# Two-layer cross attention in float32 on one core: a weight split one iteration later, the mask flag read at the end of TensorE's first iteration, and the order of the first and last iterations laid out anew

## The reference

```
# layer 0, 32 x (128 channels, 512 positions)
x_q = w_qk y;  x_k = w_qk x;  x_v = w_v x + b_v
attention = softmax(x_q^T x_k);  attention /= 1e-07 + column sums
x = x + relu(w_t (x - x_v attention) + b_t)
# layer 1, 32 x (128 rows, 512), 8 kv heads, 4 groups, head size 16
q = x Wq + bq;  k = ctx Wk + bk;  v = ctx Wv + bv
scores = q k^T / 4 + mask;  out = softmax(scores) v
x = layernorm(out Wo + bo + x) * gamma + beta
```

## Time and profile before

| | us |
|---|---|
| median of 3 runs | 802.6 |
| the three runs | 800.09, 802.60, 805.04 |
| profiled execution | 796.82 |
| its span, first to last instruction | 795.0 |
| busy: PE, DVE, POOL, ACT | 738.7, 598.1, 574.8, 479.4 |

### The profile page before, as it was taken

The page is one execution under the profiler, slowest core; times in us unless marked ns, Lnnn a source line. Parts: engine busy times, 40 slices in busy tenths (PEclk is TensorE's granted clock), DMA queues, the critical chain, the costliest instruction groups (busy, mean ns, idle before and its releaser), DMA issues.

```text
span 795.0 us, 17333 instructions
## 1 busy us (share of the span) xinstructions
PE 738.7 (93%) x5015; PEld 605.0 (76%) x5015; DVE 598.1 (75%) x1016; ACT 479.4 (60%) x1067; POOL 574.8 (72%) x770
## 2 busy tenths in 40 slices
PE   6778999999999999999999999999999999998762
PEld 5766786878878788878878788887878887886521
DVE  5676795868789596877969686878969687786742
ACT  5744747567574847657493856757484765746250
POOL 4946478686887968686896868688796868657154
PEclk9989999999999999999999999999999999999786
DMA  6524161433526152342515144342615234242510
GB/s 235 173 68 110 61 156 41 131 101 100 135 76 169 45 139 85 119 109 91 156 63 152 66 123 105 102 133 79 168 47 139 82 119 109 90 107 74 123 66 27
DMA packets 55755, 84.86 MB, mean 107 GB/s; under 512 B 9520, under 2 KB 29616, under 8 KB 55600
## 3 DMA queue, kind: packets, MB, share of 16 engines
q1 hardware_dynamic: 55008, 84.25, 36.7%
q10 hardware_dynamic: 720, 0.27, 0.2%
HBM read 24.72 MB, written 8.39 MB: 42 GB/s over the span
## 4 chain that ended last, share of the span: by engine, by line
PE 81%; DMA 7%; DVE 3%; issue 3%; POOL 3%; ACT 1%; SPq 1%; POOLq 0%; DVEq 0%; ACTq 0%
PE banks L784 8%; PE banks L875 8%; PE banks L888 6%; DMA qstack<-mrep 5%; PE banks L822 4%; PE banks L900 4%; PE banks L846 4%; PE banks L823 4%; PE banks L824 4%; PE banks L902 4%; PE banks L901 4%; PE banks L769 4%; PE banks L771 4%; PE banks L770 4%; PE banks L757 3%; PE banks L758 3%
## 5 line engine op out<-in xcount | busy, mean ns | idle before, releaser
L1526 DVE TENSOR_REDUCE maxima<-banks 128x4 f32<-128x512 f32 x256 | 160.0, 683 | 9.7 <-PE banks L846 7.7
L1183 ACT ACTIVATE prob<-banks 128x512 f32<-128x512 f32 x256 | 134.9, 608 | 40.6 <-PE banks L875 39.5
L1551 DVE RECIPROCAL dens<-dens 128x512 f32<-128x512 f32 x32 | 107.1, 3348 | 60.0 <-DMA dens<-sides 60.0
L549 POOL TENSOR_TENSOR ta<-ta,cb_s 128x516 f32<-128x516 f32 x64 | 76.5, 1197 | 100.0 <-ACT ta L1125 100.0
L784 PE MATMUL banks<-ta,att 128*128 128x130 f32 x1024 | 122.0, 278 | 3.1 <-POOL ta L556 3.1
L784 PEld LDWEIGHTS banks<-ta,att 128*128 128x128 f32 x1024 | 119.6, 193 | 5.2 <-POOL ta L556 3.3
L1117 ACT ACTIVATE att<-banks,negmax 128x512 f32<-128x512 f32 x128 | 88.7, 715 | 20.7 <-DVE negmax L1476 20.4
L1476 DVE TENSOR_REDUCE negmax<-banks 128x1 f32<-128x512 f32 x128 | 85.7, 687 | 12.4 <-PE banks L771 12.3
L875 PE MATMUL banks<-qstack,kstack 128*128 128x512 f32 x256 | 80.9, 421 | 11.7 <-DMA qstack<-mrep 11.2
L1168 ACT ACTIVATE qh<-banks,bq_s 128x256 fp32r<-128x256 f32 x64 | 30.7, 480 | 99.0 <-PE banks L824 99.0
L822 PE MATMUL banks<-x2h,wq_h 128*128 128x256 f32 x256 | 73.9, 289 | 0.7 <-POOL x2l L616 0.7
(11 more groups left out here) (145 smaller groups left out, 1972.6 us busy)
## 6 DMA issues: line engine op xcount, KB each, us to landing
qstack<-qh SPq DMA_DIRECT2D x128, 128.0 KB, 2.3
xs<-in_x SPq DMA_DIRECT2D x16, 512.0 KB, 3.6
ys<-in_ctx SPq DMA_DIRECT2D x16, 512.0 KB, 3.6
kstack<-kph SPq DMA_DIRECT2D x128, 64.0 KB, 2.0
qstack<-ql SPq DMA_DIRECT2D x64, 128.0 KB, 2.3
dens<-sides SPq DMA_DIRECT2D x64, 128.0 KB, 2.0
out_x<-late SPq DMA_DIRECT2D x32, 256.0 KB, 2.1
kstack<-kpl SPq DMA_DIRECT2D x64, 64.0 KB, 2.0
```

What stands on the lines that cost most here:

```text
L1183: nc.scalar.activation(prob[:, 2 * p + odd], banks[:, slot(plan, f"st{j}{kv}")], exp_f).then_inc(sem["prob_done"], 1)
L1526: nc.vector.tensor_reduce(maxima[:, 0, :, p, :, g].rearrange("x o j -> x j o"), banks[:, slot(plan, f"mx{g}{p}")].rearrange("x (j o s) -> ...
L1551: nc.vector.reciprocal(dens[:], dens[:]).then_inc(sem["dinv_done"], 1)
```

## The change

It has four parts. (1) out_weights_high and out_weights_low move from first_iteration(0) into iteration(1), behind x2_high and x2_low of pair 0's second half. (2) PE no longer waits for wq_ready before its branch, but before the first q_project; it reads the flag behind the last instruction of its first iteration. (3) On all engines the first iteration has a new order: both ctx_transposes first, k and v behind z, v_transpose last on PE; both scale_values ahead of split_y on POOL; query_weights_high, and on DVE k_low and setup_query_weights, at the end; the mask sums behind all exps. SP asks for the next x ahead of the mask. (4) The last iterations have two score matmuls ahead of the first values, residual_transpose of half 0 ahead of the last scores, and a few steps of ACT, POOL and DVE moved.

```diff
 FIRST_WIDE_USES = (
-    ("et0", 1), ("en00", 1), ("en01", 1), ("en02", 1), ("tva00", 1), ("tva01", 1), ("tva02", 1), ("tva03", 1),
+    ("et0", 1), ("et1", 1), ("en00", 1), ("en01", 1), ("tva00", 1), ("tva01", 1), ("tva02", 1), ("tva03", 1),
...
@@ SP first_iteration
+                if load_next:
+                    next_x(i)
                 if s1:
                     next_mask(i)
                 if load_next:
-                    next_x(i)
                     next_y(i)
@@ POOL iteration
                     x2_low(q, 1)
+                if weights:
+                    out_weights_low()
@@ POOL first_iteration
+                if s1:
+                    add_bias(i, 0, 0)
                 if split_next:
                     split_x(i + 1, 0)
-                if s1:
-                    add_bias(i, 0, 0)
+                    split_x(i + 1, 1)
+                if s1:
                     add_bias(i, 0, 1)
-                if split_next:
-                    split_x(i + 1, 1)
-                if s1:
+                    add_bias(i, 1, 0)
                     scale_values(i, 0)
-                    add_bias(i, 1, 0)
                     add_bias(i, 1, 1)
+                    scale_values(i, 1)
                 if split_next:
                     split_y(i + 1, 0)
                     split_y(i + 1, 1)
                 if s1:
-                    scale_values(i, 1)
-                if setup:
-                    out_weights_low()
-                if s1:
+                    x2_low(i, 0)
                     spread_k(i)
-                    x2_low(i, 0)
...
@@ POOL last_iteration
                     at_low(q, 0)
+                    residual_bias(q, 0)
                 if s3 and (s1 or s2):
                     scale_shift(i - 2, 1)
                 if s2:
-                    residual_bias(q, 0)
                     residual_bias(q, 1)
@@ PE q_project
                     wait(pe, "x2l_done", q, 1)
+                    if isinstance(q, int) and q == 0:
+                        pe.wait_ge(wq_ready, 1)
@@ PE
+            def setup_flag():
+                pe.wait_ge(flag_ready, 1)
+                return pe.value_load(flag_i[0:1, 0:1], min_val=0, max_val=1)
...
             first_iteration(0, FIRST, True, True, False, False, False)
-
-            pe.wait_ge(wq_ready, 1)
-            pe.wait_ge(flag_ready, 1)
-            any_mask = pe.value_load(flag_i[0:1, 0:1], min_val=0, max_val=1)
+            any_mask = setup_flag()
@@ PE last_iteration
+                    scores(q, plan, i, 1, 0, masked)
+                    scores(q, plan, i, 1, 1, masked)
                     values(q, plan, i, 0, 0)
                     values(q, plan, i, 0, 1)
-                    scores(q, plan, i, 1, 0, masked)
-                    scores(q, plan, i, 1, 1, masked)
...
+                    residual_transpose(q, plan, i, 0)
                     scores(q, plan, i, 1, 7, masked)
                     values(q, plan, i, 1, 0)
                     values(q, plan, i, 1, 1)
-                    residual_transpose(q, plan, i, 0)
@@ ACT iteration
                     x2_high(q, 1)
+                if weights:
+                    out_weights_high()
@@ ACT first_iteration
...
+                    exp_energy(i, plan, 1, 3)
+                if s0:
+                    z_high(i, plan, 0)
                 if setup:
+                    sum_masks(0)
                     sum_masks(1)
                 if s1:
                     v_biased(i, plan)
-                    exp_energy(i, plan, 1, 3)
+                if s0:
+                    z_high(i, plan, 1)
+                if s1:
+                    x2_high(i, 0)
                     k_high(i, plan)
                 if setup:
-                    out_weights_high()
                     query_weights_high()
...
@@ DVE last_iteration
                     weigh_out(i - 2, 1)
+                    residual_add(i - 2, plan, 0)
                 if s2:
                     q_low(q, plan, 0)
                 if s3:
-                    residual_add(i - 2, plan, 0)
+                    row_statistics(i - 2, 0)
...
```

More of the change, by code:

```diff
@@ L719, in _ @@
             pool.wait_ge(rows_in, 16 * 3)
-            iteration(1, True, True, False, True)
+            iteration(1, True, True, False, True, weights=True)
             iteration(2, True, True, True, True)
@@ L1019, in first_iteration @@
                 if s1:
-                    v_transpose(i, plan)
+                    kv_project(i, plan, "k", 0, "k_ps")
+                    kv_project(i, plan, "v", 1, "v_ps")
                     attend(i, plan, 0, 0)
@@ L1024, in first_iteration @@
                     attend(i, plan, 1, 1)
+                    v_transpose(i, plan)
             def last_iteration(i, plan, s0, s1, s2, s3, masked):
@@ L1354, in last_iteration @@
                 if s2:
+                    q_high(q, plan, 3)
                     exp_scores(q, plan, 0, 0)
@@ L1669, in first_iteration @@
                 if s1:
+                    energy_max(i, plan, 0, 2)
                     energy_max(i, plan, 0, 3)
-                    ctx_low(i, plan, 1)
                     energy_max(i, plan, 1, 0)
@@ L1674, in first_iteration @@
                     energy_max(i, plan, 1, 2)
+                    energy_max(i, plan, 1, 3)
                     row_inverse(i, 0)
@@ L1678, in first_iteration @@
                 if s1:
-                    energy_max(i, plan, 1, 3)
                     row_inverse(i, 1)
-                    k_low(i, plan)
+                if s0:
+                    z_low(i, plan, 0)
                 if setup:
                     setup_flag_marks()
-                    setup_flag_value()
-                    setup_query_weights()
                 if s1:
                     layer0_out(i, plan, 0)
+                if setup:
+                    setup_flag_value()
                 if s0:
-                    z_low(i, plan, 0)
                     z_low(i, plan, 1)
@@ L1692, in first_iteration @@
                     layer0_out(i, plan, 1)
+                    k_low(i, plan)
+                if setup:
+                    setup_query_weights()
             def last_iteration(i, plan, s0, s1, s2, s3, setup=False):
```

58 lines of the change are left out of this document (24 added, 34 removed), and 12 rows, old and new, of tables (FIRST_WIDE_USES, LAST_WIDE_USES).

## The result

The changed kernel takes 793.55 us (median of 11 runs, 790.35 to 798.5), the kernel before, in the same sessions, 800.11 us (11 runs, 796.47 to 806.2). The ratio is 0.9936, with a 95% interval of 0.991 to 0.9961: 5.1 us off 800, with 3.1 to 7.2 inside the interval. (The two medians alone lie 6.6 us apart; the ratio, which comes with an interval, is used from here on.) The forecast was 5.4 us less and 797.2 us, the latter because it was counted down from 802.6, the first median of three runs; on 800.1 it would have been 794.7.

The account below looks back on a forecast made before the run. TensorE, 93% busy, bounds the kernel; time can be won mainly in its first-iteration gaps. Saving 5.8 us there, less 0.4 us in the drain, gives 5.4 us off 802.6: 797.2 us, range 793.0 to 801.5.

Parts of the forecast that it names:

- the 5.8 us: First iteration: forecast saving, iteration 1 beginning at 40.3 us instead of 46.05.
- Term 2: First iteration: attend, starting at 28.2 us, runs without its 3.14 us wait for POOL's scale, nor the low clock (1.75 us).
- the 1.2 charged for the casts: First iteration: POOL loses 0.3 to 0.5 us to each of VectorE's three setup_selectors casts, 1.2 us in all.
- Term 1: Branch before iteration 1: moving the wq_ready wait saves 1.1 us; the flag's read and branch stay, 4.32 us.
- rival B: Before iteration 1: POOL not held up, branch half overlapped with PE's queue drain; 794 us, or 792; chance 0.20.
- The flag: Ahead of the branch: flag ready at 34.9 to 35.5 us, just ahead of PE's 35.95; nothing charged.
- rival A: At the branch: the flag, delayed behind Wo's load to 36.2 us, becomes the releaser; 799 us, chance 0.13.
- The covered terms: First iteration and after: later wq_l, x2_low, wo_l, kstack and x loads are ready before they are wanted; all zero.
- C: First iteration: wq_l falls behind wo_l on VectorE's turn, delaying q_project; 805 us, chance 0.05.
- 3.14 + 1.75 + 1.1: First iteration: attend's wait, its low clock and the wq_ready wait, in us, saved before 0.27 less and 0.06 plus.
- Term 3: Drain in the last iterations: two score matmuls ahead of values(0) cost +0.4 us, from -0.3 to +0.8.

Follow-up runs that it names:

- experiment 4: Kernel before with only the last iterations of the changed kernel and its LAST_WIDE_USES; 799.75 us, ratio 0.9989.
- experiment 6: Changed kernel with the side of the branch that is taken placed right behind the branch; 787.66 us, ratio 0.988.
- experiment 7: Changed kernel without reading the flag or branching, so the nonzero-mask case is left out; 788.44 us, ratio 0.9874.
- experiment 12: Kernel before with only the side for a mask without a zero flag placed right behind the branch; 793.39 us, ratio 0.9948.
- experiment 2: Kernel before with only POOL's scale_values of half 1 moved ahead of split_y; 799.63 us, ratio 0.999.
- experiment 5: Changed kernel with PE's wait for wq_ready put back ahead of its read of the flag; 797.42 us, ratio 0.9989.
- experiment 3: Kernel before with wq_ready's wait moved behind the branch and scale_values of half 1 ahead of split_y; 799.38 us, ratio 0.9982.
- experiment 8: Changed kernel with 12 and 8 constant matmuls ahead of the first scores of iterations 1 and 2; 790.39 us, ratio 0.989.
- experiment 9: Kernel before with wq_ready's wait and scale_values moved, output weights' split in iteration 1, setup_query_weights behind layer0_out; 792.87 us, ratio 0.9924.
- experiment 10: Changed kernel with the output weights' split put back into the first iteration on POOL and ScalarE; 794.84 us, ratio 0.9948.
- experiment 1: Kernel before with only PE's wait for wq_ready moved from the branch to the first q_project; 799.42 us, ratio 1.0003.

## Why the prediction came out

**The sign and size, right.** Forecast were 5.4 us off, measured 5.1 by the ratio, and the restart at 40.3 against 39.10. There is luck in how close this is: the 5.8 us were counted from a restart at 46.05, which the same order also has at 43.28 (experiment 4).

**Term 2, right in its result, 0.7 us too late.** Attend began at 27.52, forecast 28.2 within 26.2 to 30.2, with POOL's scaled `ta` and PE's own work level. The step that was off is the start of POOL's x split: I let `wkv_l` hold POOL until 18.9, but xh got in ahead of it at 17.60 and `wkv_l` waited instead (1.94 us in place of 1.22); the low part then took 2.15 in place of 1.30. That VectorE and POOL make each other wait was right, the order of the turns wasn't. From the start of xh to the scaled `ta` it was 9.86 us where 8.1 + 1.2 = 9.3 were reckoned: xh, the first xl and the scale lost 0.46, 0.85 and 0.45 us. Of the 1.2 charged for the casts only the 0.45 of the scale (1.51 instead of 1.06) came before attend; another 0.45 fell on the add_bias behind it (1.64 instead of 1.19). The 3.14 us wait and the slow clock inside attend went as said.

**Term 1, right in size, wrong in where it starts.** The issue gap was 3.96 where 4.32 was charged. Its nature I had left open; experiments 6, 7 and 12 settle that it belongs to the branch to the far side: with the wanted side right behind it nothing is left. But I added it to the end of PE's work. In the rows it counts from the semaphore that the branch waits for. From that to the restart it is 4.3 us before (`wq_l` at 41.71), 4.78 and 4.68 in experiments 2 and 5 (`wq_l`), and 4.63 after, 4.64, 4.31, 4.87 and 4.32 in experiments 3, 8, 9 and 10 (the flag), while PE's last matmul ends anywhere from 6.3 us before that semaphore to 2.6 us after it. So in experiment 9 the restart comes only 2.30 us after PE is through, at 36.00, because the flag is there at 33.43. That is rival B's reason, the branch overlapping PE's last matmuls: 0.7 us of it in the changed kernel, 2.2 and 2.6 in experiments 3 and 9. B's time, 794, is near the measured one mainly for another reason: the base, 800.1 instead of 802.6. Experiments 1 and 4 stand apart: there the second half of attend begins late, at 35.3 and 35.8, and the restart comes 8.15 and 5.44 us behind the semaphore but only 1.05 and 2.04 behind PE's last matmul.

**The flag: right in time, wrongly charged at nothing.** It was written at 34.47, forecast 34.9 to 35.5. I compared it with the end of PE's work, 35.15, and called it covered. By the rows just given the restart follows it by 4.63 us, and in experiments 3 and 9, where the flag is there at 33.30 and 33.43, the restart comes at 37.94 and 38.30, 0.8 to 1.2 us sooner than the 39.10 of the changed kernel, though PE is through later. So rival A's mechanism, the flag as releaser, is what these rows show, at a small price and not by way of Wo: Wo was asked for at 27.33 and landed 4.9 us later, the flag's DMA, asked for at 30.31, landed at about 32.4, and the flag then stood behind layer0_out on VectorE. No run moved the flag by itself, so this is a reading of rows and not an experiment.

**The covered terms, right.** `wq_l` ended at 39.90 (forecast 42.0), x2_low of half 1 at 43.03 (44.3), `wo_l` at 47.60 (48.8), 1.29 us before add_bias; the next x was asked for at 49.72 (51.4). C didn't come near. All came earlier than forecast, by 1.2 to 2.1 us. Part of the 2.1 is that `wq_l` took the turn ahead of kph and not behind it, as forecast; kph then took 3.09 us, and PE waited for neither.

**What was wrong: to whom the gain belongs.** The prediction charged 3.14 + 1.75 + 1.1 to two edits and called the reordering of VectorE and the later split "covered" at zero. Experiment 3 has exactly these two edits and no gain can be told (0.9982), 5 lacks one of them and none can be told either (0.9989); with VectorE's order and the later split added (9) everything is there (0.9924). The step that failed is reading the last wait before the restart as the bound: behind it stood a second one, z_low, ready at 44.01 us in experiment 3, which in the trace of before was ready at 45.35, ahead of the first energy at 47.07, and cost nothing there. As a forecast of the whole change the sum held, as an account of its parts it didn't.

**Term 3, right, and small.** +0.4 from the last v_transpose to the end (67.6 and 68.0), forecast +0.4; by the times no effect can be told (experiment 4). The timelines of PE and ScalarE, answering to the earlier trace rows, show ten score matmuls in one piece instead of eight:

```profile
752.20 3.42 PE L876 MATMUL banks<-qstack,kstack 128*128 128x512 f32 x10 [3.06 <-DMA qstack<-mrep]
755.55 2.62 PE L889 MATMUL banks<-prob,v 128*32 128x512 f32 x16
```

```profile
758.24 0.60 ACT L1191 ACTIVATE sides<-banks 128x512 f32<-128x512 f32 x1 [0.26 <-PE banks L889]
```

Measured from its last v_transpose that row of ScalarE starts 758.24 - 726.6 = 31.6 us on, before 758.46 - 727.4 = 31.1: 0.5 us later, near the 0.4 that was said.

**Said wrongly, without a price.** The stretch from 684.0 to 727.5 us was called a turn of the steady loop; it is iteration 15, which has no s0. A turn of the loop is 45.4 us in both kernels. PE is full in it either way (44.9 to 45.0 us). "The slow clock after the restart is the same in both" held only roughly: the mean clock of the first 4 us is 0.50 before (46 to 50 us) and 0.64 after (39.1 to 43.1). After the 2.30 us of experiment 9 there is no slow clock at all in those matmuls.

**Not foreseen.** That a lead at the restart can be lost again in one execution: in the profiled pair 0.8 of 6.95 us was left. Waits of 2 to 3 us for the stacked queries in iterations 1 to 3 differ in length and are followed by the low clock in some executions. My reckoning from restart to end assumed that the rest would take as long as before. The ratio of the runs is near that; the profiled pair isn't.

## What to carry to other kernels

Removing a wait brings back what it costs only if nothing else is late behind it: write down, for each operand of the next work, when it is ready and behind what it stands on its own engine, or the gain moves into a second wait. A long weight preparation belongs behind everything that the next stage wants on that engine, and must not overlap with a long one of the other engine that shares its turns. Where a branch stands on the critical path, put the side that is taken right behind it, and if that can't be, have what it waits for ready well before the engine's own work ends. And before a lead is read from one profile, look at a second one of the same order.

## What the runs showed of the hardware that was not expected

**A far branch costs TensorE's stream time, a near one none.** With the taken side behind the whole of the other one, the issue gap ahead of the restart that no wait explains was 4.32 us before, 3.96 after, and 3.65 (experiment 10), 3.19 (8), 2.40 (3), 2.30 (9), 2.04 (4) and 1.05 (1). With the taken side next in the program it was none (experiments 6 and 12). Counted from the semaphore that the branch waits for it is nearly constant, 4.31 to 4.87 us in eight of the ten programs; what of it lies under TensorE's last matmuls isn't seen as a gap. Why experiments 1 and 4 take longer from the semaphore is open. The Trainium skill (Runtime: NRT & Kernel Launch, section Instruction fetch mechanics) says that a taken branch to a target outside the fetched window must load it first; that agrees in kind.

**The clock after a wait of 2 to 3 us does not follow from the wait's length.** The five first scores behind such a wait took 1.40 us at the full clock or up to 2.47 at the lower level: behind 2.50, 2.92 and 2.67 us of idle time 1.40 (before, experiments 2 and 5), behind 2.94 and 1.94 us 2.47 and 2.21 (after), behind 2.25 us 2.47 (experiment 7), and in experiment 4 behind 3.36 us 1.40 and behind 2.40 us 2.47. What decides was not found.

**Turns of VectorE and POOL.** `wq_l` takes 2.28 to 2.49 us when it gets its turn at once (experiments 3, 4, 9 and 10, the changed kernel) and 6.18 when `wo_l` has the turn (before); `wo_l` itself took 6.56 us in experiments 3 and 4 behind `wq_l`, and 4.52 with the first turn. The loser of the two is whichever asks second, and in one and the same order of the first iteration it was once the one (before) and once the other (experiment 4). The Trainium skill (SBUF — State Buffer, section Who interferes with whom) has the two exclude each other for the whole instruction, and these rows agree.
